# Gathering table rows by one-hot products: a row number split into two halves of 128 and 25 high rows instead of four quarters and 13, with PSUM, signals and picks by half blocks

## The reference

```
e = leaky_relu(a_src[src] + a_dst[dst]); ee = exp(e - e_max[dst])
alpha = ee / denom[dst]; agg = segment_sum(h[src] * alpha, dst)
```

## Time and profile before

| what | us |
|---|---|
| median of 3 runs | 3728.26 (3717.64 to 3728.26) |
| the profiled execution's own time | 3704.7 |
| its span | 3703.5 |
| matrix stage, first product to last pick | 2645.7 to 3541.6 |
| mean granted TensorE clock over the span | 0.87 |

### The profile page before, as it was taken

One profiled execution on the slowest core, in us unless ns is written; L12 is line 12 of the kernel. 1 busy time (PEld: TensorE's weight loads), 2 busy tenths in 40 slices (PEclk: granted clock), 3 DMA queues, 4 the chain that ended last, 5 costly groups with the idle time before them and its releaser, 6 DMA issues.

```text
span 3703.5 us, 43100 instructions
## 1 busy us (share of the span) xinstructions
PE 2698.6 (73%) x13434; PEld 1984.5 (54%) x13459; DVE 2187.1 (59%) x5820; ACT 900.4 (24%) x1563; POOL 2365.8 (64%) x2799
## 2 busy tenths in 40 slices
PE   2565767778767777677778877777867888788935
PEld 1343545555544545455555555555646766566924
DVE  6677667777765555555455554554123757566957
ACT  3000111111112222211111111111323544344623
POOL 4666666666666666556566666668886678878040
PEclk9767979889888889889899999888978989899968
DMA  9686665666666666566666666665131112122146
GB/s 290 210 259 201 185 203 182 205 205 194 192 190 195 201 199 191 184 186 200 196 206 201 206 204 203 204 203 154 29 100 35 49 38 52 32 51 55 42 142 220
DMA packets 476802, 601.20 MB, mean 162 GB/s; under 512 B 72486, under 2 KB 415390, under 8 KB 474526
## 3 DMA queue, kind: packets, MB, share of 16 engines
q1 hardware_dynamic: 378766, 375.94, 31.3%
q0 software_dynamic: 97216, 219.88, 21.6%
q10 hardware_dynamic: 592, 2.64, 0.2%
HBM read 313.06 MB, written 286.79 MB: 162 GB/s over the span
## 4 chain that ended last, share of the span: by engine, by line
PE 28%; DVE 19%; another core or an unknown queue 14%; issue 10%; DMA 2%; ACT 1%; POOL 1%; SPq 0%; DVEq 0%; ACTq 0%; POOLq 0%
PE wide L1635 11%; PE wide L1524 7%; DVE ring L832 6%; PE wide L1584 4%; PE wide L1574 4%; DVE one_hot L765 3%; DVE picked L890 2%; DMA ring<-xn_d,srci 2%; DVE low_hot L879 1%; PE wide L1543 1%; POOL ring L1727 1%; DVE by_row L992 1%; DVE by_row L985 1%; DVE comb L1167 1%
## 5 line engine op out<-in xcount | busy, mean ns | idle before, releaser
L1727 POOL DMA_INDIRECT ring<-xn_d,srci x1611 | 1559.6, 968 | 907.6 <-issue 405.5
L832 DVE SCALAR_TENSOR_TENSOR ring<-ring,same_v,wide 128x256 f32<-128x256 f32 x1610 | 771.4, 479 | 926.5 <-remote 418.0
L1524 PE MATMUL wide<-ring,one_hot 128*128 128x256 f32 x3222 | 956.3, 434 | 374.0 <-DVE ring L832 217.0
L1524 PEld LDWEIGHTS wide<-ring,one_hot 128*128 128x128 f32 x3222 | 664.5, 216 | 625.0 <-DVE ring L832 209.0
L1635 PE MATMUL wide<-tab_parts,low_hot 128*128 128x208 bf16 x6288 | 729.8, 268 | 163.7 <-issue 149.6
L1635 PEld LDWEIGHTS wide<-tab_parts,low_hot 128*128 128x128 bf16 x6288 | 582.1, 103 | 311.5 <-issue 289.5
L1776 POOL DMA_INDIRECT g<-tab_d,srt x500 | 494.5, 989 | 82.2 <-issue 80.9
L1584 PE MATMUL wide<-w2s,hh 128*128 128x256 f32 x1568 | 417.3, 414 | 64.5 <-DVE yo L806 48.9
L1574 PE MATMUL wide<-xt,w1s 128*128 128x512 f32 (+1 forms) x832 | 407.5, 617 | 18.7 <-ACT hh L1253 15.9
L1584 PEld LDWEIGHTS wide<-w2s,hh 128*128 128x128 f32 x1568 | 325.9, 210 | 138.7 <-DVE yo L806 50.3
L1253 ACT ACTIVATE hh<-wide,b1c 128x512 f32<-128x512 f32 (+1 forms) x208 | 137.6, 662 | 1038.7 <-remote 466.3
(11 more groups left out here) (370 smaller groups left out, 1865.4 us busy)
## 6 DMA issues: line engine op xcount, KB each, us to landing
run_d<-ring SPq DMA_DIRECT2D x201, 1024.0 KB
ring<-xn_d,srci POOLq DMA_INDIRECT x1611
y_d<-yo SPq DMA_DIRECT2D x196, 128.0 KB
comb<-y_d SPq DMA_DIRECT2D x28, 896.0 KB
low_row<-low_d SPq DMA_DIRECT2D x13, 1024.0 KB
sum_d<-g SPq DMA_DIRECT2D x15, 768.0 KB
g<-tab_d,srt POOLq DMA_INDIRECT x500
xn_d<-ring SPq DMA_DIRECT2D x7, 896.0 KB, 7.0
```

Source lines behind the costliest of these rows:

```text
L832: dve_at["run", j] = step(V.scalar_tensor_tensor(out=o, in0=ring[:, (j - 1) // JC % RING, (j - 1) % JC, :], scalar=same_v[:, j:j + 1], in1 ...
L1524: mm = T.matmul(bank[pair_bank[p]][:, j % 2 * D:(j % 2 + 1) * D], one_hot[:, j // 4 % 4, j % 4, :], ring[:, j // JC % RING, j % JC, :], st ...
L1727: G.indirect_dma_start(out=ring[:, s, j % JC, :], out_offset=None, in_=xn_d, in_offset=at_rows(srci[:, j:j + 1])).then_inc(sem(f"gather{s} ...
```

## The change

A row number is split into two halves: the low part is `n & 255`, one-hot in two halves of 128 partitions, the high part `n >> 8` with 25 values. A table part has 16 x 25 = 400 columns, and an edge column takes 3 x 2 = 6 matmuls of 400 columns. All one-hots of the low part are made by ScalarE (`low_half`, still two of 512 values and four instructions for a block); VectorE's `low_columns` is gone. A column fills one PSUM bank, a half block of two columns two banks, and four half blocks are in flight (`HALF_BANK`). TensorE signals `picked` for each half block and waits for the pick of the half block four before; VectorE picks a half block (2 x 400 = 800 values) in the first and in the third step of a block. `high_hot` has 25 values for each column and is uint8. `tab_parts` is laid out by halves. `load_low` waits for ScalarE alone. The diff, cut to its core:

```diff
-BLOCK_BANK = (4, 6, 0, 2)
+HALF_BANK = (4, 6, 0, 2)
-ACT_QUARTERS = 2
+HALVES = 2
...
-    HI = -(-NT // 4)
-    LOW = 4 * P
+    HI = -(-NT // HALVES)
+    LOW = HALVES * P
+    WIDE = 4 * P
...
-    tab_parts = q.take("tab_parts", [P, 3, 4, HX, HI], BF16)
+    tab_parts = q.take("tab_parts", [P, 3, HALVES, HX, HI], BF16)
...
-    high_hot = r.take("high_hot", [P, NTC, HI], BF16)
+    high_hot = r.take("high_hot", [P, NTC, HI], U8)
...
-    low_hot = q.take("low_hot", [P, DEPTH, 4, LOW], BF16)
-    picked = q.take("picked", [P, 4, HX, HI], F32)
+    low_hot = q.take("low_hot", [P, DEPTH, HALVES, WIDE], BF16)
+    picked = q.take("picked", [P, 2, HX, HI], F32)
...
-            for b in range(AHEAD):
-                low_columns(b)
-            yield
-
-        def low_columns(b):
-
-            c = chunk_of[b]
-            V.wait_ge(sem(f"low_in{c % 2}"), sent(c // 2))
-            if b >= DEPTH:
-                V.wait_ge(sem("picked"), b - DEPTH + 1)
-            at = block_in[b] * LOW
-            for q_ in range(4 - ACT_QUARTERS):
-                dve_at["low_hot", b] = step(V.tensor_scalar(low_hot[:, b % DEPTH, q_, :], low_row[:, c % 2, at:at + LOW],
-                                                            lane[:, q_:q_ + 1], None, ALU.is_equal))
-
-        def pick(b):
...
+        def pick(b, h):
+            m = 2 * b + h
+            c, k = chunk_of[b], pool_cols[chunk_of[b]] + block_in[b] * 4 + 2 * h
+            V.wait_ge(sem("picked"), m + 1)
...
+            first = HALF_BANK[m % 4]
+            dve_at["taken", m] = then(V.tensor_tensor(
                 picked[:, :, :, :],
...
+                wide[:, first:first + 2, 0:HX * HI].rearrange("p k (f h) -> p k f h", h=HI),
+                high_hot[:, 2 * m:2 * m + 2, None, :].broadcast_to([P, 2, HX, HI]), ALU.mult))
+            dve_at["pick", b, h] = step(V.tensor_reduce(g[:, c % GR, k:k + 2, 0:HX], picked[:, :, :, :], AXX, ALU.add))
...
         def matrix_gathers():
             for b in range(NBLOCKS + 1):
                 if b >= 1:
-                    pick(b - 1)
-                yield
-                if b + AHEAD < NBLOCKS:
-                    low_columns(b + AHEAD)
-                yield
+                    pick(b - 1, 0)
+                yield
+                yield
+                if b >= 1:
+                    pick(b - 1, 1)
+                    dve_at["pick", b - 1] = dve_at["pick", b - 1, 1]
                 yield
                 yield
...
                         if i == 0:
-                            T.wait_ge(dve_step, dve_at["low_hot", b])
-                            T.wait_ge(sem("low_quarter"), ACT_QUARTERS * (b + 1))
+                            T.wait_ge(sem("low_half"), HALVES * (b + 1))
...
-                            if b >= DEPTH:
-                                T.wait_ge(dve_step, dve_at["taken", b - DEPTH])
-                        at = i % 2 * (2 * P)
+                        m = 2 * b + i // 2
+                        if i % 2 == 0 and m >= 4:
+                            T.wait_ge(dve_step, dve_at["taken", m - 4])
                         for k in range(3):
-                            for q_ in range(4):
+                            for q_ in range(HALVES):
...
-                        if i == 3:
+                        if i % 2:
                             mm.then_inc(sem("picked"), 1)
```

More of the change, by code:

```diff
@@ L9 @@
 I16 = mybir.dt.int16
+U8 = mybir.dt.uint8
 I32 = mybir.dt.int32
@@ L284, in build @@
     q = Region(r3)
-    low_hot = q.take("low_hot", [P, DEPTH, 4, LOW], BF16)
-    picked = q.take("picked", [P, 4, HX, HI], F32)
-    far_off = q.take("far_off", [P, 2, ACT_QUARTERS, LOW], F16)
+    low_hot = q.take("low_hot", [P, DEPTH, HALVES, WIDE], BF16)
+    picked = q.take("picked", [P, 2, HX, HI], F32)
+    far_off = q.take("far_off", [P, 2, HALVES, WIDE], F16)
     assert q.at <= r5
@@ L745, in sort_steps @@
             yield
-            for k, (op, by) in enumerate(((ALU.bitwise_and, LOW - 1), (ALU.logical_shift_right, 9))):
+            for k, (op, by) in enumerate(((ALU.bitwise_and, LOW - 1), (ALU.logical_shift_right, LOW.bit_length() - 1))):
                 for c0, c1 in ((0, NCF - WIDE_CHUNKS), (NCF - WIDE_CHUNKS, NCF)):
@@ L849, in split_table @@
             left = whole
-            then(V.memset(tab_parts[:, :, :, :, NT // 4:HI], 0.0))
+            then(V.memset(tab_parts[:, :, :, :, NT // HALVES:HI], 0.0))
             for k in range(3):
@@ L854, in split_table @@
                 o = tab_parts[:, k, :, :, :].rearrange("p q f h -> p h q f")
-                full = NT // 4 * 4
-                step(V.tensor_copy(o[:, 0:NT // 4, :, :], left[:, 0:full, :].rearrange("p (h q) f -> p h q f", q=4)))
-                then(V.tensor_copy(o[:, NT // 4, 0:NT - full, :], left[:, full:NT, :]))
+                full = NT // HALVES * HALVES
+                step(V.tensor_copy(o[:, 0:NT // HALVES, :, :],
+                                   left[:, 0:full, :].rearrange("p (h q) f -> p h q f", q=HALVES)))
+                then(V.tensor_copy(o[:, NT // HALVES, 0:NT - full, :], left[:, full:NT, :]))
                 if k < 2:
-                    step(V.tensor_copy(tab_part[:, 0:full, :].rearrange("p (h q) f -> p h q f", q=4),
-                                       o[:, 0:NT // 4, :, :]))
-                    then(V.tensor_copy(tab_part[:, full:NT, :], o[:, NT // 4, 0:NT - full, :]))
+                    step(V.tensor_copy(tab_part[:, 0:full, :].rearrange("p (h q) f -> p h q f", q=HALVES),
+                                       o[:, 0:NT // HALVES, :, :]))
+                    then(V.tensor_copy(tab_part[:, full:NT, :], o[:, NT // HALVES, 0:NT - full, :]))
                     then(V.tensor_tensor(tab_rest[:, :, :], left, tab_part[:, :, :], ALU.subtract))
@@ L866, in split_table @@
             yield
[L867 to L884 removed]
+        def pick(b, h):
+            m = 2 * b + h
+            c, k = chunk_of[b], pool_cols[chunk_of[b]] + block_in[b] * 4 + 2 * h
+            V.wait_ge(sem("picked"), m + 1)
             if c >= GR:
                 V.wait_ge(sem(f"sum_out{c % GR}"), sent(c // GR - 1))
[L887 to L890 removed]
+            if m >= 1:
+                V.wait_ge(dve_step, dve_at["pick", (m - 1) // 2, (m - 1) % 2])
+            first = HALF_BANK[m % 4]
+            dve_at["taken", m] = then(V.tensor_tensor(
                 picked[:, :, :, :],
[L892 to L895 removed]
+                wide[:, first:first + 2, 0:HX * HI].rearrange("p k (f h) -> p k f h", h=HI),
+                high_hot[:, 2 * m:2 * m + 2, None, :].broadcast_to([P, 2, HX, HI]), ALU.mult))
+            dve_at["pick", b, h] = step(V.tensor_reduce(g[:, c % GR, k:k + 2, 0:HX], picked[:, :, :, :], AXX, ALU.add))
         def matrix_gathers():
@@ L1338, in scalar_program @@
                 for b in range(AHEAD):
-                    low_quarter(b)
+                    low_half(b)
             done += 1
             if done % 4 == 2 and done // 4 + AHEAD < NBLOCKS:
-                low_quarter(done // 4 + AHEAD)
+                low_half(done // 4 + AHEAD)
             if done in weighed_at:
@@ L1941, in load_low @@
             if c >= 2:
-                Q.wait_ge(dve_step, dve_at["low_hot", last_block[c - 2]])
-                Q.wait_ge(sem("far_off"), ACT_QUARTERS * (last_block[c - 2] + 1))
+                Q.wait_ge(sem("far_off"), HALVES * (last_block[c - 2] + 1))
             Q.dma_start(low_row[:, c % 2, 0:tensor_cols[c] * P],
```

34 lines of the change are left out of this document (12 added, 22 removed).

## The result

The kernel after takes 3624.07 us (median of its runs, 3619.11 to 3632.65) against 3722.95 us for the kernel before (3701.86 to 3728.26). The medians lie 99 us apart. The ratio is 0.9747, with a 95% interval of 0.9701 to 0.9793, so the kernel after is 2.5% faster. The forecast was 151 us and 3577 us.

The account below looks back on a forecast made before the run. TensorE bounds the stage, by pauses beside GpSimd's gathers. 119, 600 and 22 us make 741 in place of 896, 155 less; with 4 us more before it, 151 less: 3577 us from 3728.3, range 3535 to 3645.

Parts of the forecast that it names:

- a fixed rate of instructions: TensorE, matrix stage: instructions arrive at 4.42 pairs per us beside gathers, so half the pairs take 5.43 us a block.
- the clock's case: Rival, matrix stage: TensorE's clock drops while it waits for VectorE, 97 us less plus 4, 3635 us; chance 0.1.
- the allowance: Matrix stage: 22 us (3%), ends 0 and 60, for VectorE waiting as TensorE may lead by only two blocks.
- First 22 blocks: Matrix stage before any chunk is weighed: 5.43 us a block in place of 10.9, 119 us in all.
- the 68 free matmuls: Earlier trace: 68 matmuls ran without a pause after a 0.61 us wait of TensorE, read as stocked instructions.
- Array-time rival: Rival, matrix stage: pauses are array time, a paused block takes 10.3 us, total about 3735 us; chance 0.1.
- Late blocks: Matrix stage from the 23rd block on: VectorE bounds at 5.5 us a block, 109 blocks 600 us.
- The start of the stage: Before the matrix stage: the larger `high_hot` takes 6.5 us more on VectorE, counted as 4 us, ends 0 and 6.5.
- GpSimd: Matrix stage: its 48.93 us wait for chunk 0's sums goes, and its gathers end near 3340, a floor.
- ScalarE: Matrix stage: still two one-hots, 2.8 us a block, within 202 us of idle time; cost nothing.
- Behind the last pick: After the matrix stage: what follows the last pick, 162 us, stays unchanged.
- The uint8 rival: Rival, VectorE's product: uint8 operand takes two cycles per element, 7.2 us a late block, 3760 us; chance 0.05.

Follow-up runs that it names:

- a_two_picked: The kernel after with two buffers for VectorE's products, so none waits for the sum before it; 3518.21 us on the second chip (kernel before there 3547.03).
- a_n200: The kernel after with five of each six matmuls cut to 200 columns, as many instructions; 3633.61 us on the first chip.
- a_pause100: The kernel after with GpSimd's memset between gathers cut from 280 to 100 elements; 3901.37 us on the second chip (kernel before there 3547.03).
- b_nogather: The kernel before without GpSimd's indirect DMAs and pauses in the matrix stage, one memset a chunk instead; 3381.96 us on the first chip (kernel before there 3725.22).
- b_memsets: The kernel before with three more memsets in place of each of GpSimd's gathers; 3578.86 us on the first chip (kernel before there 3725.22).

## Why the prediction was right, and where its size was off

The direction and the new bound were right, and so was the cause in its main part: half the pairs lose less time beside the gathers, and VectorE is the bound behind block 22. What was wrong in the mechanism is the form of the loss, a fixed rate of instructions. Of the forecast 151 us, 85 came in the profiled execution. That 3624 us lies in the forecast's range of 3535 to 3645 is in part luck: its upper end was set by the clock's case and by the upper end of the allowance, and neither came; other terms were missed, and nearly all of them the same way. The missing 66 us by the forecast's own terms:

- **First 22 blocks: forecast 119 us, measured 142.0, +23.** This is the step that failed. I read the earlier trace rows as a supply of 4.42 pairs per us and kept it (5.43 us a block). The supply was not fixed: it was 3.40 pairs per us with longer matmuls, 7.06 us a block in that stretch and 6.69 in the mean of blocks 3 to 22. The table above puts an added 0.12 us a pair in its place: 24 x (0.169 + 0.125) = 7.1, against 10.9 for 48 old pairs. The pauses did not halve in number with the pairs: by the counts above they went from 9.1 to 5.9 a block, since they keep step with the gathers and a block takes less time. With the 68 free matmuls as my evidence I had a stock of instructions, and from it wrongly concluded a rate.
- **Array-time rival: refuted in its strong form.** It asked for 10.3 us a block. It was nearer to the truth than I gave it credit for in one thing: on this chip a pair's own array time does not hide under its pause.
- **Late blocks: forecast 5.5 us each, 600 in all; measured 5.91, 644, +44, against an allowance of 22 for the whole stage.** In the slots of VectorE from 2860 to 3350 us the picks take 4.01 us a block (forecast 3.87) and the chunk's work 1.79 (1.62). The first excess is the hand-over from a sum to a product that follows at once, 1.12 us in 63 of 168 cases in place of 0.90. `a_two_picked` shows that the hand-over is the wait for the sum right before. Of the second excess about a third is that the stretch of 24.9 blocks that I took for the mean held less than its share: its chunk work is 1.86 us a block in summed durations, and 1.92 over all later blocks of before. The rest of it is not traced. The two make 5.80; what is left is 0.11 a block or 12 us, where I had allowed 22. The waits of VectorE's picks from 2812 us on are less than that:

```profile
DVE picked L880 <- remote: 3.0, 2, 1.7
DVE picked L880 <- PE wide L1624: 0.9, 1, 0.9
DVE picked L880 <- DVE g L884: 0.5, 1, 0.5
DVE picked L880 <- issue: 0.2, 1, 0.2
```

  They add up to 4.6 us. Another 6 us are no waiting at all: behind 2812 us VectorE still has a block and a half of the first 22 to pick. So the lead of two blocks in PSUM costs some 5 us here.
- **The start of the stage: forecast +4 us, measured +24.5.** Making `high_hot` now takes this:

```profile
L755 DVE TENSOR_TENSOR high_hot<-iota_b,digit_f x1: 13803/13803/13803, 1579.1 to 1579.1; 128x13100 uint8<-128x13100 bf16 x1
```

  13.80 us in place of 7.25, 6.55 more, as forecast, and it is absorbed: the 961st gather of the first stage, which lies ahead of it, is already 9.2 us later than in the profile of before, and the 1021st, behind it, 9.7 us. The rest builds up to 20.9 at the last gather, in instructions that the diff does not touch. That looks like drift between two executions: those of before lie up to 26 us apart, and on the first chip the stage began at 2651.9 and 2659.4 us in the two variants of before and at 2652.3 and 2675.6 in the two of after. By the medians the kernels are 99 us apart, not 85.
- **GpSimd: right.** The wait for sums went, and the last gather began at 3375.1; forecast was near 3340, and with the later start 3365. It is 81 us ahead of the last pick, so GpSimd's end was no bound on this chip.
- **ScalarE: right.** 262 one-hots of 709 ns, each preceded by less waiting, 89.2 us of idle time in place of 202.0. **Behind the last pick: right**, 161.9 us in both.
- **The uint8 rival: refuted**, 986 ns for 800 values. **The clock's rival: refuted here**, 1.00 and 0.98 in the two stretches. The Trainium skill (TensorE: Matmul & The Clock Gate, Why this matters for your kernels) warns of idle gaps between bursts of matmuls. After kept the clock; `a_n200` did not in its early stretch (0.51), nor did `a_pause100` (0.66). The concern is borne out by those two runs, though not by the change itself, and in `a_n200` by short gaps alone: from 2695 to 2827 us TensorE's longest idle time was 0.8 us.

```profile
PE wide L1625 <- issue: 32.6, 82, 0.8
```

The sum closes: 23 + 44 - 22 = 45 us in the stage (785.9 against 741) and 20.5 at its start make 66.

The Trainium skill's statement that TensorE waits for no other engine at its memory ports (SBUF — State Buffer, Who interferes with whom) is not contradicted as it stands, but the conclusion that GpSimd's work is therefore free for TensorE is: `b_nogather` and the kernel before differ by 329 us in the stage, and 4.42 pairs per us with gathers become 11.2 without. `b_memsets` agrees with the page, since GpSimd's writes alone hardly slow TensorE.

**What stays open.** What the indirect DMAs share with TensorE's instructions is not shown: the trace has only "issue". Whether it is the issuing on GpSimd or the transfer behind it was not tried apart. The fetch of instructions from memory doesn't look like it: the page of before counts 108 packets of the instruction queue in the whole span, and the pauses come every 1.46 us. Whether the loss belongs to the pair or to the gather, and why it is there on one chip, looks like a fixed supply on the second and is nothing on the third, is open too. The kernel after in its own form was not profiled on the second chip, and the longer pause was not tried on the first, where it might pay. No version was run that beats both kernels on all three chips. That `a_two_picked` helps on the first chip is likely from the slots (63 x 0.2 us in 500 us), but was not tried.

## What to carry to other kernels

Before you trade one engine's work for another's, ask what the time that you remove is made of: here it was idle time beside another engine's indirect DMAs, and TensorE's own work hardly fell. Run once a kernel that leaves the suspected cause out (`b_nogather`), and you know how much there is to win and what the change costs without it. And where a gain comes from a disturbance, measure it on more than one chip: this one is a gain of 2.5% on a chip with the disturbance and a loss of 0.5% on one without.

## What the runs showed of the hardware that I had not expected

- Indirect DMAs issued by GpSimd slow the stream of matmuls on TensorE, with idle time that has no releaser and keeps step with the gathers (on the result's chip 78 of 102 pauses ended 0.2 to 0.4 us behind the start of one): 4.42 pairs of 208 columns per us beside gathers at 1.46 us, 11.2 without, 10.5 beside as much GpSimd work by memsets.
- The effect depends steeply on the distance of the gathers: with a memset of 0.20 us between them in place of 0.35, gathers 1.31 us apart and not 1.46, a pair of 400 columns went from 0.17 to 1.31 us on the second chip (0.43 in a mean that takes in GpSimd's waits).
- It depends on the chip, as far as one chip of each kind can tell. The same kernel before took 3725, 3547 and 3152 us; with the old shape a pair took 0.226, 0.161 and 0.089 us (the third with the slightly longer pause), at an equal busy share of GpSimd (89%). The stages ahead of the matrix stage differ as well: it starts near 2650, 2620 and 2290 us.
- On VectorE a product that waited for the sum right before it started about 0.2 us later than one that did not (1.12 against 0.90 us from start to start).
